# Attention scores in column groups of 32 keys, and squares of two units in one VectorE instruction

## What is computed

```python
scores = jnp.einsum('bhqd,bhkd->bhqk', q, k) * hs ** (-0.5)
p = jax.nn.softplus(scores)
p = p * p
causal = jnp.tril(jnp.ones((t, t), dtype=p.dtype))
p = p * causal
attn = p / (jnp.sum(p, axis=-1, keepdims=True) + 1e-09)
out = jnp.einsum('bhqk,bhkd->bhqd', attn, v)
```

## Time and profile before

| | us |
|---|---|
| median of 3 runs | 1607.56 (1599.33 to 1610.26) |
| the profiled execution | 1605.87 |
| its span | 1604.0 |
| matmuls of TensorE busy | 1520.9 |
| VectorE busy | 1216.4 |
| ScalarE busy | 873.0 |
| GpSimd busy | 411.4 |

### The profile page before, as it was taken

The page is one execution under the profiler, slowest core; times in us unless marked ns, Lnnn a source line. Parts: engine busy times, 40 slices in busy tenths (PEclk is TensorE's granted clock), DMA queues, the critical chain, the costliest instruction groups (busy, mean ns, idle before and its releaser), DMA issues. The chain is left out here.

```text
span 1604.0 us, 28965 instructions
## 1 busy us (share of the span) xinstructions
PE 1520.9 (95%) x11188; PEld 1125.0 (70%) x11188; DVE 1216.4 (76%) x2334; ACT 873.0 (54%) x1372; POOL 411.4 (26%) x382
## 2 busy tenths in 40 slices
PE   8999898999999998999989999979999999899998
PEld 7888776444444446888867778756777777678777
DVE  4554797898999986664578888768777777688886
ACT  3333387988888886332332222278888887321220
POOL 0002111222122224100433221113555555211111
PEclk9999999999999999999999999999999999999999
DMA  4000065777777750000100000022333333100000
GB/s 159 26 1 14 20 188 178 100 95 106 106 101 102 100 72 2 14 1 1 40 27 8 1 1 1 1 69 78 102 101 107 106 107 107 40 14 27 14 27 27
DMA packets 57160, 95.83 MB, mean 60 GB/s; under 512 B 7904, under 2 KB 29632, under 8 KB 57024
## 3 DMA queue, kind: packets, MB, share of 16 engines
q1 hardware_dynamic: 56064, 93.38, 26.4%
q10 hardware_dynamic: 960, 0.59, 0.1%
HBM read 76.91 MB, written 17.04 MB: 59 GB/s over the span
## 5 line engine op out<-in xcount | busy, mean ns | idle before, releaser
L1438 DVE TENSOR_TENSOR att_weights<-att_weights 128x1024 f32<-128x1024 f32 (+1 forms) x224 | 267.7, 1241 | 39.4 <-ACT att_weights L1411 39.1
L928 DVE SCALAR_TENSOR_TENSOR X<-ps,moe_gsel,X 128x256 f32<-128x256 f32 x512 | 246.1, 483 | 63.5 <-PE ps L48 41.1
L1411 ACT ACTIVATE att_weights<-ps 128x1024 f32<-128x1024 f32 (+1 forms) x288 | 264.9, 992 | 39.8 <-PE ps L1347 20.5
L48 PE MATMUL ps<-w_experts_hi,moe_xh 128*128 128x512 f32 x512 | 205.1, 401 | 1.1 <-DVE X L928 1.1
L48 PE MATMUL ps<-w_experts_hi,moe_xl 128*128 128x512 f32 x512 | 203.3, 397 | 0.0
L48 PE MATMUL ps<-w_experts_lo,moe_xh 128*128 128x512 f32 x512 | 201.6, 394 | 0.0
L1367 PE MATMUL ps<-att_weights,att_v_ones 64*32 64x64 f32 (+5 forms) x2048 | 157.6, 400 | 0.0
L424 ACT ACTIVATE ffn_gates<-ps,ffn_gate_bias 128x512 f32<-128x512 f32 x72 | 49.5, 688 | 148.3 <-PE ps L48 126.6
L48 PEld LDWEIGHTS ps<-w_experts_hi,moe_xh 128*128 128x128 f32 x512 | 96.2, 188 | 27.9 <-DVE X L928 4.5
L48 PEld LDWEIGHTS ps<-w_experts_lo,moe_xh 128*128 128x128 f32 x512 | 96.1, 188 | 22.1
L48 PEld LDWEIGHTS ps<-w_experts_hi,moe_xl 128*128 128x128 f32 x512 | 96.3, 188 | 20.3
(11 more groups left out here) (281 smaller groups left out, 3672.1 us busy)
## 6 DMA issues: line engine op xcount, KB each, us to landing
ssm_lb<-decays SPq DMA_DIRECT2D x32, 512.0 KB, 4.7
ssm_rise<-decays SPq DMA_DIRECT2D x28, 512.0 KB, 3.9
qk_parts<-qkv_part SPq DMA_DIRECT2D x32, 384.0 KB, 2.8
q_stack<-qk_parts SPq DMA_DIRECT2D x64, 128.0 KB, 4.6
k_stack<-qk_parts SPq DMA_DIRECT2D x64, 128.0 KB, 7.8
att_q_stack<-qk_parts SPq DMA_DIRECT2D x64, 128.0 KB, 4.8
att_k_stack<-qk_parts SPq DMA_DIRECT2D x64, 128.0 KB, 8.8
out<-X SPq DMA_DIRECT2D x7, 512.0 KB, 2.9
```

What stands on the lines that cost most here:

```text
L48: ins = pe.matmul(out, l(k), r(k), start=first and n == 0, stop=last and n == len(passes) - 1)
L928: dve.scalar_tensor_tensor(out=x, in0=ring[:, e // 2, (e % 2) * C:(e % 2 + 1) * C], scalar=gsel[:, s, j, e:e + 1], in1=x, op0=ALU.mult, op ...
L1411: act.activation(Wt[:, u % WU, 0:n], scores(u)[:, 0:n], ACT.Softplus).then_inc(p_done, 1)
L1438: dve.tensor_tensor(wt, wt, wt, ALU.mult).then_inc(sq_done["dve"], 1)
```

## The change

- `KG` = 32: each product of scores with 128 keys is split into four matmuls of 32 keys, each into its own 32 partitions of PSUM; one with 64 keys into two. A mask is now two matmuls of 32 keys, for the two groups of keys that have one, and not one for all 128. An UPPER unit's bank is set by four matmuls of 128 rows and 32 columns.
- The matmul that set O's bank before block 0 is gone; the first products of that block start the accumulation.
- Where two units of one step are both squared by VectorE, it takes them in one instruction over both places of `Wt`, 2048 columns, at the second of the two units (`wide`, `in_wide`, `finishes`). Per pass these are (0,1), (2,3), (7,8), (9,10), (13,14) and (15,16).
- ScalarE squares units 5, 6 and 12 in place of 6, 9 and 14. `squares` counts the instructions accordingly.

```diff
--- before.py
+++ after.py
@@ -1281,13 +1281,19 @@
     STEPS_AHEAD = 4
     TURN_LAG, COPY_LAG, DEN_LAG, OUT_LAG = 2, 7, 9, 10
     SU, WU = 3, 12
+    KG = 32
     assert NU % SU == 0 and NU % WU == 0
-    BY_ACT, BY_POOL = (6, 9, 14), (11,)
+    BY_ACT, BY_POOL = (5, 6, 12), (11,)
     squarer = ["act" if u % PU in BY_ACT else "pool" if u % PU in BY_POOL else "dve" for u in range(NU)]
+    wide = [squarer[u] == "dve" and u + 1 < NU and squarer[u + 1] == "dve" and step_of[u] == step_of[u + 1] and u % WU != WU - 1
+            for u in range(NU)]
+    in_wide = [wide[u] or u > 0 and wide[u - 1] for u in range(NU)]
+    finishes = [not wide[u] for u in range(NU)]
 
     def squares(by, i, u):
 
-        return i * squarer.count(by) + squarer[:u + 1].count(by)
+        done = [x for x in range(NU) if squarer[x] == by and finishes[x]]
+        return i * len(done) + sum(x <= u + wide[u] for x in done)
 
     def outputs_at(x, ends, n, lag, i, first, stage):
 
@@ -1333,18 +1339,21 @@
                 upper = segments[0][-1] == UPPER
                 pe.wait_ge(p_done, i * NU + u + 1)
                 if upper:
-                    low = slice(0, HALF)
                     pe.sem_inc(scores_free, 1)
-                    for r in range(2):
-                        pe.matmul(scores(u)[r * HALF:(r + 1) * HALF, 0].rearrange("p (s q) -> p s q", q=HALF), neg[low, low],
-                                  ident16[low, low].unsqueeze(1).broadcast_to([HALF, BANK // HALF, HALF]), start=True, stop=False)
+                    for g in range(P // KG):
+                        at = g * KG % HALF
+                        pe.matmul(scores(u)[g * KG:(g + 1) * KG, 0].rearrange("p (s q) -> p s q", q=HALF), neg[:, at:at + KG],
+                                  ident16[:, 0:HALF].unsqueeze(1).broadcast_to([P, BANK // HALF, HALF]), start=True, stop=False)
                 for n, (h, kj, t, c, q, w, part) in enumerate(segments):
-                    rows = slice(h % 2 * HALF, (h % 2 + 1) * HALF) if part == UPPER else slice(0, P)
-                    keys = slice(kj * P, kj * P + (HALF if part == UPPER else P))
-                    ins = pe.matmul(scores(u)[rows, t, c:c + w], SK[s][:, h, keys], SQ[s][:, h, q:q + w],
-                                    start=not upper, stop=n >= len(segments) - 2 if upper else part == FULL)
+                    groups = range(h % 2 * HALF, (h % 2 + 1) * HALF, KG) if part == UPPER else range(0, P, KG)
+                    for g in groups:
+                        keys = kj * P + (g % HALF if part == UPPER else g)
+                        masked = part == REST and g >= HALF
+                        ins = pe.matmul(scores(u)[g:g + KG, t, c:c + w], SK[s][:, h, keys:keys + KG], SQ[s][:, h, q:q + w],
+                                        start=not upper, stop=n >= len(segments) - 2 if upper else not masked)
                     if part == REST:
-                        ins = pe.matmul(scores(u)[:, t, c:c + HALF], neg[:, :], ident16[:, HALF:P], start=False, stop=True)
+                        for g in range(HALF, P, KG):
+                            ins = pe.matmul(scores(u)[g:g + KG, t, c:c + HALF], neg[:, g:g + KG], ident16[:, HALF:P], start=False, stop=True)
                 ins.then_inc(s_done, 1)
 
             def value_step(i, m):
@@ -1354,8 +1363,6 @@
                     pe.wait_ge(v_copied, 2 * (2 * i + s + 1))
                 if products[0][1] == 0 and not upper:
                     pe.wait_ge(o_done, (i * 2 + s) * BLOCKS + qb + 1)
-                    if qb == 0:
-                        pe.matmul(O(qb), ident16[:, :], neg[:, 0:1].broadcast_to([P, BANK]), start=True, stop=False)
                 for u in step_units[m]:
                     pe.wait_ge(sq_done[squarer[u]], squares(squarer[u], i, u))
                 if upper:
@@ -1365,7 +1372,7 @@
                     rows = slice(h % 2 * HALF, (h % 2 + 1) * HALF) if part == UPPER else slice(0, P)
                     values = va_up[rows, s, kj, h // 2] if part == UPPER and h % 2 else va[rows, s, kj, h]
                     ins = pe.matmul(O(qb)[h * 2 * HD:(h + 1) * 2 * HD, q0:q0 + w], values,
-                                    Wt[rows, (s * PU + unit) % WU, t, c:c + w], start=kj == 0 and part == FULL, stop=part == UPPER and kj == (qb + 1) * GT - 1)
+                                    Wt[rows, (s * PU + unit) % WU, t, c:c + w], start=kj == 0 and part != UPPER, stop=part == UPPER and kj == (qb + 1) * GT - 1)
                 ins.then_inc(pv_done, 1)
 
             def turn_output(n, i, k):
@@ -1434,7 +1441,7 @@
         def _(dve):
             def square(i, u):
                 dve.wait_ge(p_done, SU + i * NU + u + 1)
-                wt = Wt[:, u % WU, 0:BANKS[u % PU]]
+                wt = Wt[:, u % WU - 1:u % WU + 1] if in_wide[u] else Wt[:, u % WU, 0:BANKS[u % PU]]
                 dve.tensor_tensor(wt, wt, wt, ALU.mult).then_inc(sq_done["dve"], 1)
 
             def copy_output(n, i, k):
@@ -1461,7 +1468,7 @@
 
             def body(i, first=False, last=False):
                 for u in range(NU):
-                    if squarer[u] == "dve":
+                    if squarer[u] == "dve" and finishes[u]:
                         square(i, u)
                     outputs_at(u, BLOCK_UNITS, NU, COPY_LAG, i, first, copy_output)
                     outputs_at(u, BLOCK_UNITS, NU, DEN_LAG, i, first, invert_sums)
```

## The result

| | us | ratio to before, 95% interval |
|---|---|---|
| before | 1606.2 (1599.3 to 1610.3, 4 runs) | |
| after | 1650.8 (1648.1 to 1652.2, 4 runs) | 1.028 (1.024 to 1.032) |

The changed kernel is 45 us slower. The forecast was 1668 (1612 to 1712), so sign and range hold.

The account below looks back on a forecast made before the run. TensorE was taken to set the 21.3 us pass of attention; saved work, late instruction packets and lower clock made it 25.1, so 16 x 3.8 = +61: 1605.9 + 61 + 1.7 = 1668 us, range 1612 to 1712.

Parts of the forecast that it names:

- the groups' gain: TensorE in attention: fewer tile-size changes (-1.36 us) and no O clearing (-0.21) cut its work per pass from 20.5 to 18.9.
- By that alone: TensorE's saved work without late instructions: a pass of 19.8 us instead of 21.3, 16 x -1.5 = -24, 1584 us.
- Instructions and packets: TensorE's loads and matmuls rise from 570 to 992 per pass; their 16 KB packets come late during data bursts, leaving holes.
- Rival A: TensorE's instruction fetch stays hidden: pass 19.8 us, 1584 us in all; chance 0.13.
- then gets one each 8.4: In a 15.5 us data burst TensorE gets an instruction block each 8.4 us: 2.06 blocks per burst, pass 24.6 us.
- the ten latencies: Times from a packet's edge to the next packet's possible use, read from the earlier trace: 2.8 to 10.2 us.
- The clock: TensorE runs at the lower clock after a long hole: 1.7 us of work lost, 0.5 us per pass taken.
- a pair's first unit is ready a softplus and 1.1 us later; its values are four steps of scores away, which covers that, so nothing: Pairing VectorE's squares delays a pair's first unit; four steps of scores before its values cover this, so no cost.
- the line on ScalarE's three squares: ScalarE keeps three squares per pass, now units 5, 6, 12, and GpSimd one; no cost was given.
- rival C: The oT copies stand behind a 2.2 us pair; both transposes wait 0.5 us per pass: 20.8 us, 1600; chance 0.08.
- Rival B: Small weight loads show on TensorE: up to 0.7 us per pass, +5 us; chance of costing beyond the range 0.04.
- The signs to look for: Attention about 410 us, "issue" holes of 2 to 6 us in bursts, lower clock after some, value step 0.86 us before scores.

Follow-up runs that it names:

- the kernel before, paced: Kernel before the change, with its 16 stack transfers per pass issued one per unit of scores instead of all at once; 1598.3 us, 0.996.
- the changed one with both stalls gone: Changed kernel, first block's O copied two units earlier, stacks loaded one transfer per unit (1583.9 us) or, from the third pass, a quarter of their bytes (1583.0 us).
- groups alone: Changed kernel with squares as before: one unit per instruction, ScalarE's units 6, 9, 14; groups of 32 keys stay; 1625.3 us, 1.013.
- groups of 64 keys: Kernel before with scores in groups of 64 keys, O's clearing gone, old squares, stack transfers all at once; 1601.7 us, 0.998.
- a quarter of the data: Changed kernel, but stack loads from the third pass on bring one head of four; 1654.1 us, 1.031.
- squares alone: Kernel before with the wide squares and ScalarE's units 5, 6, 12; scores in 128 keys and O's clearing stay; 1669.9 us, 1.040.
- squares with the copy earlier: Kernel before with wide squares and ScalarE's units 5, 6, 12, the first block's copy of O two units earlier; 1607.3 us, 1.001.
- ScalarE's units moved: Kernel before with only ScalarE's squares changed, units 5, 6, 12 for 6, 9, 14; 1637.9 us, 1.020.
- copy earlier, quarter of the data: Changed kernel, first block's copy of O two units earlier, stack loads from the third pass on bringing one head of four; 1583.0 us, 0.986.

## Why the prediction was right or wrong

**What bounds the kernel, and the groups' gain: right.** The prediction had 20.5 - 1.6 = 18.9 us of TensorE's work per pass, 25 us less in all. Busy time at the same clock is 332.2 in the kernel before, paced, and 307.7 in the changed one with both stalls gone, 24.5 less. "By that alone" 1584; measured 1583.0 and 1583.9. That this meets so closely is in part luck. The pass is 20.12 us and not 19.8, since the transposes now wait 1.2 us for the copy of the second block, which the forecast had not; and against the kernel before with pacing as well the whole gain is 14 us (1598.3 to 1583.9). The other 6 are the holes and the clock of the kernel before, which pacing takes away.

**Instructions and packets: right in kind.** 26 more were forecast and 26 came; holes of 0.7 to 4.9 us stand 256 apart in bursts of data, some 3.2 us behind the start of a packet, and nearly all of them go with the data or with pacing (1.4 us are left when paced). Rival A (fetch hidden, 1584) has fallen: 38 us lie bare in groups alone. The Trainium skill takes its side (Runtime: NRT & Kernel Launch, Instruction fetch mechanics: mostly hidden); these runs agree only where no burst of data stands in the way.

**Their size: too dear.** The failing step is "then gets one each 8.4", 2.06 blocks in a burst and a pass of 24.6. In groups alone, where the other stall is small, 17 of some 62 blocks end in a hole of over 0.6 us and last 7.9 us in the mean. That length is near the forecast's 8.4, but there are 1.1 such blocks per pass where 1.56 were forecast, and a block without a hole does not always run at 4.76 us, so less of the 7.9 is hole. The holes sum to 38 / 16 = 2.4 us per pass, where 24.6 - 19.8 = 4.8 was forecast. A long block (8.4 to 10.8) is mostly followed or led by shorter ones of 4 to 7.4, and the ten latencies held time in which no packet was awaited, as groups of 64 keys show. The clock went the other way: 0.5 us per pass was taken, and it is (326.9 - 304.6) / 16 = 1.4. Fetches and clock together are 3.8 per pass and not 5.3. Beside the holes, the waits for softplus and the copy shrink from 27.2 to 14.7 us, 0.8 per pass, for which the forecast had no term. So holes and all that goes with them cost 374.7 - 331.1 = 43.6 us and not 16 x 5.3 = 85, and the groups come to +21 us and not +61.

**The squares: wrong.** The step is "a pair's first unit is ready a softplus and 1.1 us later; its values are four steps of scores away, which covers that, so nothing", and beside it the line on ScalarE's three squares, which put no price on 5, 6, 12 for 6, 9, 14. The values are indeed covered. But the copy of O is queued behind the squares on VectorE, and TensorE has no cover for that one. Alone this part costs 64 us, beside the groups about 25. The prediction had named the place as rival C and dismissed it by the 0.8 us that the earlier trace rows show, at 0.5 us twice a pass. Where nothing hides it, it is 3.4 once a pass, and near 2 of clock behind it. The rows were there: the earlier trace rows are VectorE at this place. What was missing was to list VectorE's queue from ScalarE's squares to the copy, before and after.

**The sum: in range by luck.** A term too dear and a term left out made up for each other. Between the two kernels TensorE's idle time in attention grows by 49.4 us and its busy time shrinks by 2.0: 24.5 less of work, 22.5 more from the lower clock (332.6 - 307.7 = 24.9 against 334.6 - 332.2 = 2.4). 49.4 - 2.0 = 47.4. By my sorting, whose gaps are a little longer than the idle time, 31 are edges and 24 the copy, and softplus has 2 less. The forecast had 61 for the first alone. Rival B, small loads, has fallen: a pass of 20.12 us is the 18.9 of TensorE's work and the 1.2 of the copy, and nothing is left for them. In the same kernel 28 small scores of an upper unit, each with its own load, start 15 ns apart, so four take 60 ns and not the 107 that rival B estimates (24 sets at 107 ns are 2.6 us, not 2.7).

**The signs to look for** came as told but for the size: waits on "issue", in holes of 0.7 to 4.9 us for 2 to 6, the clock at 0.50 behind holes, attention longer (396 for 410), and the value step at 0.87 ahead of scores.

## What to carry to other kernels

An instruction that is moved or widened on an engine must be priced for all that is queued behind it there; here a copy of 0.68 us was what TensorE needed next. Two stalls that can hide each other must both be taken away before a gain is seen: here taking the holes away won nothing (1654), moving the copy 23 us, and both together 67. A stream of small instructions needs its own instructions delivered, so large loads go out one at a time and not in a burst.

## What the runs showed of the hardware

- Instruction packets of 256 are delayed by bursts of data on the DMA engines and not by the same bytes spread out: 39.4 us of holes at edges in attention with 16 transfers at once, 1.4 with one per unit.
- A wait of TensorE of 3.36 us was followed by the lower clock for about 3.4 us (0.50, 0.56), in 15 of 15 passes with a quarter of the data. The same length is no sure sign: with squares alone it was so after 6 of the 11 waits of 3.2 us. The waits of 1.2 us were not followed by it in any pass (0.99 over the whole stretch), while one hole of 1.4 us was (squares with the copy earlier, from 376.6 us). With ScalarE's units moved it followed 6 of the 11 waits of 2.15 us, one of which is (windows from the wait on):

```profile
478.20:480.35 2.15, 0.15 (x5) 0.01 (x1) 2.15 (x3) 2.05 (x3) 2.09 (x3) 1.00 0.00 0
480.35:482.05 1.70, 1.70 (x15) 1.41 (x16) 1.67 (x4) 0.13 (x1) 1.33 (x1) 0.72 0.00 0
482.05:483.75 1.70, 1.70 (x15) 0.71 (x14) 1.70 (x3) 1.66 (x2) 0.00 (x0) 0.50 0.00 0
483.75:485.50 1.75, 1.75 (x30) 0.58 (x26) 1.72 (x2) 0.29 (x2) 0.00 (x0) 0.79 0.00 0
```

- A VectorE square that starts within a GpSimd square takes longer by nearly the whole overlap: 1.0 us for an overlap of 1.1 (before), 1.6 for 1.7 (after), 1.7 for 1.8 (ScalarE's units moved). Where VectorE's started first, GpSimd's was the longer one, 3.4 us for 1.9.
- Matmuls of 64 columns with a load of 32 columns each started 15 ns apart, side by side in four column groups (copy earlier, quarter of the data).
